# Attention in a two-layer block on one core: the value products' accumulator gets a second PSUM bank, the score ring gives one up

## The reference

```python
x = x + 0.5 * L0_ffn(layernorm(x))          # 2 experts, top 1
x = x + L0_attn(layernorm(x))               # the stage that is changed
x = x + 0.5 * L0_ffn(layernorm(x))
x = x + 0.5 * L1_ffn(layernorm(x))          # 8 experts, top 2
x = x + L1_attn(layernorm(x))               # state-space mixer
x = x + 0.5 * L1_ffn(layernorm(x))

def L0_attn(x):                             # s = 1024, H = 16, DK = 16
    Q, K, V = (proj(W, b) for W, b in ((Wq, bq), (Wk, bk), (Wv, bv)))
    scores = einsum('bhqd,bhkd->bhqk', Q, K) / DK ** 0.5
    scores = where(key > query, -inf, scores)
    ctx = einsum('bhqk,bhkd->bhqd', softmax(scores), V)
    return einsum('bsd,ed->bse', ctx, Wo) + bo
```

## Time and profile before

| | us |
|---|---|
| median of 3 runs (1069.8 to 1074.49) | 1070.07 |
| the profiled execution's own time | 1079.51 |
| its span, from the first instruction to the last | 1077.6 |
| PE (TensorE) busy | 872.3 (81%) |
| DVE (VectorE) busy | 596.7 (55%) |
| POOL (GpSimd) busy | 496.7 (46%) |
| ACT (ScalarE) busy | 350.5 (33%) |

### The profile page before, as it was taken

How to read it: one execution, slowest core, us unless ns; L and a number is a source line. 1 busy time by engine, 2 the same in 40 slices (tenths; PEclk the granted TensorE clock), 3 DMA queues, 4 the chain that set the end, 5 groups by cost and what they waited for, 6 DMA issues and landing times.

```text
span 1077.6 us, 21037 instructions
## 1 busy us (share of the span) xinstructions
PE 872.3 (81%) x7576; PEld 547.5 (51%) x7577; DVE 596.7 (55%) x1147; ACT 350.5 (33%) x811; POOL 496.7 (46%) x538
## 2 busy tenths in 40 slices
PE   2089936878887968997759999958679987899995
PEld 1046622322222233664449899823424444699994
DVE  4723336666686353333635455477389865654555
ACT  2422201144553601221205444315701122344441
POOL 2228867068887021111234554222389852445541
PEclk9999978997898997999859999979999999899998
DMA  8213442345554351001676666251000001666654
GB/s 300 87 45 117 123 127 69 133 132 189 167 163 163 146 199 30 26 25 35 238 284 225 204 240 228 88 160 49 0 1 0 1 1 40 228 234 222 227 201 132
DMA packets 48454, 142.21 MB, mean 132 GB/s; under 512 B 11345, under 2 KB 24418, under 8 KB 41858
## 3 DMA queue, kind: packets, MB, share of 16 engines
q0 software_dynamic: 19280, 93.40, 25.7%
q1 hardware_dynamic: 24090, 42.88, 11.2%
q10 hardware_dynamic: 5016, 4.98, 1.3%
HBM read 106.11 MB, written 35.16 MB: 131 GB/s over the span
## 4 chain that ended last, share of the span: by engine, by line
PE 60%; DVE 14%; DMA 10%; POOL 6%; issue 4%; ACT 4%; SPq 1%; another core or an unknown queue 0%; ACTq 0%; DVEq 0%; POOLq 0%
PE psum L553 14%; PE psum L526 11%; PE psum L512 7%; PE psum L1283 6%; PE psum L1751 4%; DVE mem L1384 3%; DMA mem<-w2l_dram 2%; POOL mem L236 2%; PE psum L1258 2%; PE psum L186 2%; PE psum L114 2%; DMA max_dram<-mem 1%; PE psum L499 1%; DMA mem<-max_dram 1%; PE psum L1778 1%
## 5 line engine op out<-in xcount | busy, mean ns | idle before, releaser
L553 PE MATMUL psum<-mem 128*128 x1536 | 179.5, 273 | 5.3 <-DVE mem L791 2.5
L553 PEld LDWEIGHTS psum<-mem 128*128 128x128 f16 x1536 | 146.2, 98 | 26.4 <-issue 7.4
L526 PE MATMUL psum<-mem 128*128 128x128 f16 x2208 | 134.5, 220 | 0.4 <-issue 0.4
L902 POOL DMA_INDIRECT y_dram<-mem x64 | 64.0, 1001 | 148.8 <-DVE mem L807 145.8
L643 ACT ACTIVATE mem<-psum,mem 128x128 f32<-128x128 f32 x368 | 105.1, 371 | 82.2 <-PE psum L526 43.9
L526 PEld LDWEIGHTS psum<-mem 128*128 128x128 f16 x2208 | 128.8, 99 | 2.9 <-issue 1.3
L897 POOL DMA_INDIRECT mem<-xn_dram,mem x64 | 65.1, 1017 | 114.0 <-PE psum L499 89.6
L1384 DVE TENSOR_REDUCE mem<-psum 128x2 f32<-128x1024 f32 (+2 forms) x96 | 89.1, 951 | 48.4 <-PE psum L1236 24.9
L1342 ACT ACTIVATE mem<-psum 128x512 f32<-128x512 f32 (+1 forms) x160 | 80.0, 552 | 93.9 <-PE psum L1258 49.9
L512 PE MATMUL psum<-mem 128*128 x432 | 102.1, 396 | 0.8 <-issue 0.8
L1283 PE MATMUL psum<-mem 128*17 128x512 f32 (+3 forms) x384 | 85.4, 544 | 16.7 <-DVE mem L1403 16.7
(11 more groups left out here) (247 smaller groups left out, 1445.2 us busy)
## 6 DMA issues: line engine op xcount, KB each, us to landing
stage<-in_w POOLq DMA_DIRECT2D x20, 480.0 KB
stage<-in_w POOLq DMA_DIRECT2D x16, 512.0 KB
w_rows<-mem SPq DMA_DIRECT2D x4, 2048.0 KB, 15.7
w2h_dram<-mem POOLq DMA_DIRECT2D x20, 240.0 KB, 2.3
w2l_dram<-mem POOLq DMA_DIRECT2D x20, 240.0 KB, 3.0
xn_dram<-mem ACTq DMA_DIRECT2D x32, 128.0 KB, 1.7
mem<-w2h_dram SPq DMA_DIRECT2D x2, 2048.0 KB, 14.0
mem<-w2l_dram SPq DMA_DIRECT2D x2, 2048.0 KB, 19.7
```

The costliest lines, as they stand in the source:

```text
L526: ins = eng.matmul(c.bank(2 * p + j // half)[:, j % half * P:(j % half + 1) * P], mats[q][:, l, k, j * P:(j + 1) * P], x[:, p, k, :], star ...
L553: ins = eng.matmul(c.bank(6)[:, 0:D], a[:, 0 if gated else p, q * half + j, :], w[:, at], start=(i == 0), stop=(i == 3 * CF - 1))
L902: eng.indirect_dma_start(c.y_dram[:, :], bass.IndirectOffsetOnAxis(ap=yidx[:, b:b + 1], axis=0), yo[:, b % 2, :], None).then_inc(s_ys[b % ...
```

## The change

Product and transpose use bank 6 for even pairs and bank 7 for odd ones, so `product(p, 0)` waits for the transpose of pair p - 2 and no longer for that of pair p - 1. Score tiles use two banks, 4 for the first head and 5 for the second; `scores` waits for both exponentials of the step ahead, where it waited for the first of them only. The zeroing covers two banks. The `keep_awake` matmuls at the stage's start write bank 4, where they wrote 6. No instruction is added, removed or moved on any engine's queue. The diff, whole:

```diff
@@ -1213,7 +1213,7 @@
-        keep_awake(c, eng, 6, 12)
+        keep_awake(c, eng, 4, 12)
@@ -1244,11 +1244,9 @@
-            if at >= 3:
-                eng.wait_ge(*s_ex(at - 2))
-            if at + 1 >= 3:
-                eng.wait_ge(*s_ex(at - 1))
-            outs = [c.bank(4 + (at + j) % 3) for j in range(2)]
+            if at:
+                eng.wait_ge(*s_ex(at))
+            outs = [c.bank(4 + j) for j in range(2)]
@@ -1272,14 +1270,14 @@
-            if i == 0 and p:
-                eng.wait_ge(*s_tn(p))
+            if i == 0 and p >= 2:
+                eng.wait_ge(*s_tn(p - 1))
...
-                    out = c.bank(7)[32 * (2 * s + j):32 * (2 * s + j) + VW, a - s * BANK:a - s * BANK + w]
+                    out = c.bank(6 + p % 2)[32 * (2 * s + j):32 * (2 * s + j) + VW, a - s * BANK:a - s * BANK + w]
@@ -1287,8 +1285,8 @@
-            keep_awake(c, eng, 6, 2)
-        keep_awake(c, eng, 6, 12)
+            keep_awake(c, eng, 4, 2)
+        keep_awake(c, eng, 4, 12)
@@ -1339,7 +1337,7 @@
-                    eng.activation(pt[:, (p * NS + i) % RING, j, 0:w], c.bank(4 + (at + j) % 3)[:, 0:w], ACT.Exp,
+                    eng.activation(pt[:, (p * NS + i) % RING, j, 0:w], c.bank(4 + j)[:, 0:w], ACT.Exp,
@@ -1353,7 +1351,7 @@
-        eng.memset(c.bank(7), 0.0)
+        eng.memset(c.banks(6, 2), 0.0)
@@ -1400,7 +1398,7 @@
-            eng.transpose(tn[:, :, :].rearrange("p b c -> p (b c)"), c.bank(7)).then_inc(s_tn.sem, 1)
+            eng.transpose(tn[:, :, :].rearrange("p b c -> p (b c)"), c.bank(6 + p % 2)).then_inc(s_tn.sem, 1)
```

## The result

Timed in alternation with the kernel before, the changed kernel took 1080.97 us (median of 13 runs, 1072.36 to 1084.97), the kernel before 1072.79 us (13 runs, 1066.57 to 1080.79): a ratio of 1.0057, interval 1.0030 to 1.0083 (the two medians divided would give 1.0076). A second measurement of the same code, beside which the kernel before took 1080.97 us, gave 1.0003, 0.9966 to 1.0040 (experiment 2). The two together show no gain and leave a cost between nothing and 0.8%, an effect about as large as what a measurement of this kernel can tell.

What follows compares the result with a forecast made beforehand. TensorE held 60% of the chain, with the maxima's round trip behind the transpose wait. Accumulator -5.4, score ring +6.1, zeroing +0.5 and clock -1.0 made +0.2 us: 1070.3 us on 1070.07, range 1060 to 1079.

Steps and rivals of the forecast that it cites:

- The naive gain of the removed wait: Rival for pairs: the product's stall goes in full, maxima not binding step 3; 16 us, 1054 us, 7 in 100.
- the maxima's round trip: Pairs, step 3: can only move up to the landing of the maxima's second half; pairs 1, 4, 5, 7 gain 0.
- The ring's steps: Score steps with two banks: at least 1.63 us plain, 1.72 in steps 0 and 7, 1.81 in 1 and 8.
- +2.8 us in pairs 1 to 6: Steps 5 to 8 of these pairs lose 0.46 us each time, six times, through the two-bank score ring.
- The zeroing: Accumulator zeroing, on the chain with 0.48 us, covers twice the columns: +0.5 us.
- the small idles of the two-bank ring: Rival in steps 3 to 8: TensorE's 0.1 us idles bring 1.2 GHz; 17 us, 1087 us, 8 in 100.
- Term 1: Accumulator's wait, step 0 to step 3: pairs 2, 3 and 6 gain 0.9, 2.1 and 2.4 us; -5.4 in sum.
- term 2: Score ring: +1.1 us in pair 0, +2.8 in pairs 1 to 6, the rest in pair 7; +6.1 in sum.
- one sign of being wrong that the prediction named: A window over steps 5 to 9 showing a granted clock under 1 would mean the kernel is slower.
- Term 4: TensorE's clock in pairs 3 and 6: stays up in one of the two, -1.0 us, bounds 0 and -2.

Runs made afterwards that it cites:

- experiments 3 and 4: GpSimd's split held back until the last scores, in the kernel before (ratio 1.1111, pairs 147.2 us) and in the changed kernel (1.0998, pairs 136.9 us).
- experiment 1: Kernel before with the score ring cut to two banks and nothing else, one accumulator bank kept: ratio 1.0051.
- experiment 4: Changed kernel with GpSimd's split held back until the last scores: ratio 1.0998, pairs 136.9 us.
- experiment 8: Changed kernel with GpSimd's split started two steps later, so that its chunks fall elsewhere against the pairs: ratio 0.9967.
- Experiments 5, 6 and 11: Changed kernel with normalisation's second half later, 0.9981; with last maxima piece a step earlier, 1.0063; with that piece, all normalisation late and zeroing moved, 0.9913.
- experiments 6 and 12: Changed kernel with the last maxima piece a step earlier, 1.0063; with pieces at old steps, all normalisation late and zeroing off the chain, 1.0037.
- experiment 7: Kernel before with GpSimd's split started two steps later, so that its chunks fall elsewhere against the pairs: ratio 1.0025.

## Why the prediction held, and where it did not

The forecast was 1070.3 us on 1070.07, no change that can be told, in a range of 1060 to 1079. By the ratio of 1.0057 the measured time is 1076 us on the same base: in the range, at the slower side; the second measurement would give 1070.4. In the traced pairs -0.3 us was forecast and +0.5 measured. That nearness is in part luck: the way from step 0 to step 3 came out 3.8 us better than forecast, the rest of pairs 1 to 6 4.9 us worse, and the two misses nearly cancel.

**What held.** The naive gain of the removed wait, 16 us, did not come, and for the stated reason: behind the transpose stood the maxima's round trip (TensorE now idles at step 3 of each of pairs 1 to 6 until the transfer lands; and in experiments 3 and 4, without the load, the change is worth 10 us). The ring's steps came to within 0.01 us, steps 3 to 9 of pair 0 and the whole of pair 7 to within 0.1; timed alone the ring cost 5.5 us of the 6.1 forecast, with an interval from 1.3 to 9.6. Its +2.8 us in pairs 1 to 6 shows in no trace as a sum (experiment 1). The zeroing cost its 0.5 us. The clock did not fall for the small idles of the two-bank ring, in any trace: the pairs of experiment 4, with such a step throughout, have 1.00 over 136.89 us.

**Term 1, too small.** Step 0 to step 3 of pairs 1 to 6 fell by 9.2 us in the trace (8.7 in the second), not 5.4. Three pairs were counted; the trace has five that gained and one (pair 1, 9.24 to 10.44) that lost, as the landing did not stay where it had been. It was taken as fixed against step 0, but in pairs 4 and 5, where gain 0 was counted, it came 2.2 and 2.0 us earlier. The place of a round trip in GpSimd's chunks alone moves single pairs of the changed kernel by 0.3 to 3.4 us (experiment 8).

**The step that failed** is in term 2: "steps 3 and 4 stay bounded by TensorE, so they lose nothing. What is left is steps 5 to 8: ... = 0.46". It looked at ScalarE as the only partner of these steps. The second partner is VectorE, whose order is the next maxima, then `normalise(p - 1)`. Taking TensorE's wait away moved TensorE forward against VectorE, and the wait turned up two steps later, in step 5, where the maxima's eighth piece needs the banks of the sixth. Step 3 to the next step 0 cost 6.7 us over the six pairs (4.9 in the second trace), not 1.8, and with the low clock behind it this, with the ring's 3 us in pairs 0 and 7, ate what term 1 gave. Without GpSimd's load the wait in step 5 cost only 2.0 us (experiment 4); with it, 6.6 and 3.9 in the two traces. Experiments 5, 6 and 11 show the wait go away in all pairs but pair 5, deepen, and move on, as VectorE's order and TensorE's lead are changed. So one sign of being wrong that the prediction named did appear, a granted clock under 1 over steps 5 to 9 (0.75 in pair 2, 0.85 in pair 4), but behind that wait, not by the ring's small idles.

**Term 4.** Counted as one pair in which the clock stays up; pair 6 as a whole has 1.00 (0.84 before), pairs 3 and 5 have 0.92 (0.84 and 0.85 before), and pairs 2 and 4 fell to 1.2 GHz in step 6 and not in step 3. So its sign was right, and its place hung on the wait that was missed.

**Open.** The two traces of the changed kernel are 2.4 and 2.5 us longer than the one of the kernel before, of which the change explains 0.5 in the zeroing and -1.1 to +0.5 in the pairs; the 13 timed runs say 6 us, the 12 later ones 0.3. With such a spread the size, between nothing and 0.8%, stays open. Why experiments 6 and 12, and the unshifted and the shifted kernels, differ in their traced pairs by more than in their ratios was not found out either; each has one trace. Nor was it tried what the kernel before gains from a VectorE order of its own.

## What to carry to other kernels

A second buffer removes a wait only as far as the next one behind it, and it also moves the engine that waited forward against all its other partners. So after pricing the wait, walk the next few steps on each partner's queue: here VectorE's order, made for a late TensorE, and GpSimd's load beside it cost most of what the bank had given. Once that order and the last maxima piece were moved, the kernel with the bank was 0.8% faster than the kernel before. And what is bought with the bank has a price that can be read off before: a ring of two makes producer and consumer take turns, and a step is then the sum of both and of the hand-over.

## What the hardware showed beyond that

Casts and two-input operations of VectorE on data in SBUF can be held up for many times their length beside GpSimd's: joining 16 partial maxima a partition took 0.17 us, and 1.58 and 2.03 us in pairs 1 and 6 of the changed kernel; the cast 0.43 and 2.35, the subtraction 0.69 and up to 2.46. In all twelve traces with GpSimd's loop beside the pairs, each VectorE instruction there that took well over its shortest time overlaps an operation of GpSimd's (1.8 to 2.4 us each), and with GpSimd still (experiments 3 and 4) none took longer. Reciprocals (0.25 us) and transposes (0.71 us) kept their length throughout, and so did the reductions from PSUM: the longest took 1.23 us in both kernels, with GpSimd's loop and without.

The write of 8 KB of maxima to HBM takes 1.4 us at the least in both kernels and up to 9.6 us before and 8.5 us after. With GpSimd still it took up to 5.6 and 6.0 us, so the load is not the only cause; what else delays it was not looked into.

The executions of one kernel with GpSimd's loop beside the pairs spread over 1.0 to 2.4%. The traced execution of experiment 7 took 1075.9 us, the median of its timed runs 1086.8. A single trace of such a kernel gives the mechanism, not the size.
